# Attention with narrow products in double groups and three banks for each kind of scores, and a shorter gating search, lists and beginning

## The chip, the cores and the metric

The kernel runs on one core of a Trainium2 chip. The metric is the device time of one execution in microseconds (us). A core has a matrix engine (TensorE; PE in the profile, its weight loads PEld), a vector engine (VectorE, DVE), an activation engine (ScalarE, ACT), a general one (GpSimd, POOL), and a queue engine (SyncE, SP) that mostly issues DMAs. Each runs its own instructions in order and they meet only through semaphores. The matrix engine writes to eight banks of PSUM, 512 float32 numbers a partition each.

## The reference

Two layers over `x` of 16 x 256 x 512, with `ctx_2048` of the same shape: a long convolution over the context that stands for the first attention, a mixture of 32 small experts gated once per batch entry, a true attention, and a mixture of 8 experts with the two best for each row.

```
x = x + tanh(g_xattn[0]) * L0_xattn(ctx, ctx, layernorm(x), ssm_kernel, D, 8)
x = x + tanh(g_ffn[0])   * L0_ffn(layernorm(x), sim_matrix, gates, w_q, w_k, w_v, o_weights)
x = x + tanh(g_xattn[1]) * L1_xattn(layernorm(x), ctx, ctx)
x = x + tanh(g_ffn[1])   * L1_ffn(layernorm(x), w_router, w_fc, w_proj)

L0_ffn gating:  logits = affinity - sigmoid(gates); mask = relu(logits) > 0
                if no expert is active: the mask is that of the 16 largest logits of 32
                routing = softmax(where(mask > 0, gated, -max))
L1_xattn:       qk = einsum('bdm,bdn->bmn', qh, kh) / sqrt(32)   # 128 heads, each 512 x 512
                ret = einsum('bmn,bcn->bcm', softmax(qk), vh)
L1_ffn:         two best of 8 experts a row; y = square(relu(x @ w_fc[e])) @ w_proj[e], weighted
```

## The kernel before

The program runs as five stages: layer norm and transposes; the convolution as products with Toeplitz blocks; the gating and first experts; the attention with the routing of its rows; and the second experts, 71 tiles of 128 rows gathered by expert. The change touches three of them.

**Gating** (end of the third stage). DVE makes the logits of 16 batch entries and 32 experts, and finds which are among the 16 largest by comparing all pairs: five operations over 16x1024 (`over`, `same`, `rank`, L908 to L912). POOL made the triangle `later` for ties. From the mask come `rm` and `RB`, and PE's products L805 combine the experts' output weights, which SP loads at L610. PE runs a filler, `stir(pe, pk[5], 34)`, products with the identity that nothing reads, in the meantime.

**Attention.** The work is 32 units, each of four heads of 512 x 512. `unit_loop` runs `body(j, i, u)` with eight units written out and the rest as a loop of four. In a unit PE issues, in 16 beats, one *second* score product (L1463, keys against queries with the maxima as two more rows, 98 deep, for unit j) and one *first* score product (L1445, 96 deep, for a unit ahead, by `ahead` with `LEAD = 5` pairs of tiles). First scores go to `pA`, two pairs of banks: DVE takes the negated maximum over two tiles at once (`reduce`, L1817), so a pair of banks is free when its one reduction is. When all 16 are in, POOL splits the maxima in a high and a low part (`halves`), PE turns them (`maxima`, L1454) at beat `TURN = 10`, ACT copies them (`keep`, L1661), and SP moves them into two rows of the queries (`shift`, L1251), which unit j+1 needs at its first beat. Second scores go to `pB`, two banks in turn (`bank`); ACT takes the exponential of each (L1710) into `pt`, and the product two places on waits for it. There are 17 places a unit in that ring (`RING`), 16 seconds and the turned maxima. POOL adds three of the four key blocks of `pt` (L1399, L1404).

The *narrow* products are 32 columns wide, four heads side by side: `values` (L1473) for each of four key blocks, and `sums` (L1486) with ones, once over POOL's part sums and once over the last block. Each is a group of four products and is put by hand at a beat: values 0 at 13, values 1 at 15, and in the next unit values 2 at 2, sums at 5 and 7, values 3 at 10.

The beginning: SP loads keys, queries and values of units 0, 1 and 2 (six loads of 256 KB and a value tile of 256 KB each) on one queue; PE runs a filler of 32, then all 16 first scores of unit 0 and 10 of unit 1; SP's queue holds the shift of unit 0 behind these loads.

**Lists** (behind the attention). DVE picks the two best experts of each row in four groups, PE counts, and then eight chunks make the slot lists: DVE's `where` (L1934) and `what` (L1939), ACT's scaled copies (L1764), PE's sums (L1606). Ahead of them DVE makes the picks' weights (`weights`). Then ACT copies the first expert's weights (`fc_at`, L1771), SP having loaded all of them, and the tiles begin.

## Time and profile before

| | us |
|---|---|
| median of 3 runs | 1626.49 (1622.04 to 1628.45) |
| the profiled execution | 1629.35 |
| its span | 1627.3 |
| PE busy | 1538.0 (95%) |
| DVE busy | 1193.8 (73%) |
| POOL busy | 1032.7 (63%) |
| ACT busy | 980.1 (60%) |
| mean granted clock of PE | 0.978 |

The page shows each engine's busy time, the span in 40 slices, the DMA queues, the chain of work that ended last, and the costliest groups of instructions. A chain names, step by step, what released the work; with `<-` a row names the releaser of an idle time. The attention lies between about 525 and 1037 us of the span, the gating's end about 437 to 454, the lists about 1090 to 1118. Matmul ends are modelled, so a product's listed duration is longer than the distance to the next one's start; distances between starts are what counts.

### The profile page before, as it was taken

How to read it: one execution, taken by the hardware profiler on the slowest of the kernel's cores; microseconds unless marked ns; L12 is line 12 of the kernel's file. 1: busy time of each engine (PE TensorE's matmuls, PEld its weight loads, DVE VectorE, ACT ScalarE, POOL GpSimd, SP SyncE). 2: the span in 40 equal slices, each digit the busy share in tenths (PEclk: the TensorE clock that was granted, in tenths of full speed). 3: DMA queues.
4: the chain of work that ended last, by engine and by line, in shares of the span. 5: the costliest groups of instructions: out<-in, count | busy, mean ns of one | idle time of the engine just before them, and what ended most of it. 6: DMA issues, size and time to landing. Idle time of an engine off the chain costs nothing.

```text
span 1627.3 us, 28669 instructions
## 1 busy us (share of the span) xinstructions
PE 1538.0 (95%) x8969; PEld 1080.2 (66%) x8969; DVE 1193.8 (73%) x1869; ACT 980.1 (60%) x1529; POOL 1032.7 (63%) x855
## 2 busy tenths in 40 slices
PE   5999999998897999999999999888999999999996
PEld 4677777777653644444444444368999999999995
DVE  7688888888837677777777777166777777777774
ACT  6333333333724378888888887637667767777773
POOL 4788888885406588888888887501555555555553
PEclk9999999999998999999999999989999999999998
DMA  7244444445763967777777772491444444444443
GB/s 256 97 132 137 142 142 142 142 132 130 197 186 100 199 167 194 189 184 204 183 187 201 186 188 75 155 328 36 79 75 79 79 74 75 78 77 78 79 79 52
DMA packets 110843, 224.27 MB, mean 138 GB/s; under 512 B 12704, under 2 KB 12704, under 8 KB 109856
## 3 DMA queue, kind: packets, MB, share of 16 engines
q1 hardware_dynamic: 94848, 185.88, 40.4%
q0 software_dynamic: 15904, 37.23, 13.2%
q8 instruction: 49, 0.80, 0.2%
q14 instruction: 42, 0.34, 0.1%
HBM read 146.71 MB, written 75.84 MB: 137 GB/s over the span
## 4 chain that ended last, share of the span: by engine, by line
PE 38%; DMA 20%; issue 3%; DVE 3%; ACT 2%; POOL 1%; SPq 0%; ACTq 0%; POOLq 0%; DVEq 0%
DMA out_rows<-XN,slots 18%; PE pB L1463 10%; PE pO L1473 8%; PE pA L1445 7%; PE pO L1486 4%; PE pA L1624 3%; PE pO L1636 3%; DMA XN<-normed_rows,slots 1%; PE pB L1454 1%; PE pA L1541 1%; DVE low L1817 1%; POOL out_rows L1429 1%; PE pA L1614 1%; DMA qs<-q_low 1%; PE pA L1548 0%
## 5 line engine op out<-in xcount | busy, mean ns | idle before, releaser
L1817 DVE TENSOR_REDUCE low<-pA 128x2 f32<-128x1024 f32 x256 | 306.9, 1223 | 113.2 <-PE pA L1445 99.5
L1710 ACT ACTIVATE pt<-pB 128x512 f32<-128x512 f32 x512 | 287.6, 594 | 88.4 <-PE pB L1463 80.2
L436 PE MATMUL y<-kv,toep 128*128 128x288 f32 x1280 | 327.8, 413 | 9.1 <-DVEq L63 5.8
L1429 POOL DMA_INDIRECT out_rows<-XN,slots x71 | 195.2, 2749 | 211.9 <-DMA out_rows<-XN,slots 172.8
L436 PEld LDWEIGHTS y<-kv,toep 128*128 128x128 f32 x1280 | 239.1, 191 | 97.6 <-DVEq L63 34.1
L1624 PEld LDWEIGHTS pA<-XN,fc 128*128 128x128 f32 x2272 | 264.3, 192 | 7.9 <-issue 2.6
L1624 PE MATMUL pA<-XN,fc 128*128 128x128 f32 x2272 | 265.1, 275 | 2.0 <-issue 1.0
L1463 PE MATMUL pB<-qs,ks 98*128 98x512 f32 x512 | 226.8, 446 | 3.4 <-ACT pt L1710 2.4
L1463 PEld LDWEIGHTS pB<-qs,ks 98*128 98x128 f32 x512 | 95.3, 188 | 193.5 <-ACT pt L1710 150.5
L406 ACT ACTIVATE ym<-y 128x384 f32<-128x384 f32 (+1 forms) x128 | 52.6, 411 | 230.6 <-PE y L436 230.6
L1776 ACT ACTIVATE proj_high<-WP 128x2048 fp32r x71 | 135.7, 1912 | 81.2 <-PE pO L1636 81.2
L1445 PE MATMUL pA<-ks,qs 96*128 96x512 f32 x512 | 182.6, 399 | 0.5 <-DMA qs<-q_low 0.3
L1992 DVE TENSOR_TENSOR proj_low<-WP,proj_high 128x2048 fp32r<-128x2048 f32 x71 | 162.8, 2292 | 8.1 <-ACT proj_high L1776 3.0
L1399 POOL TENSOR_TENSOR part_sum<-pt 128x1024 f32<-128x1024 f32 x64 | 152.2, 2378 | 21.8 <-ACT pt L1710 16.0
L1404 POOL TENSOR_TENSOR part_sum<-part_sum,pt 128x1024 f32<-128x1024 f32 x64 | 152.6, 2385 | 6.9 <-POOL part_sum L1399 3.8
L1473 PE MATMUL pO<-pt,vt 128*32 128x512 f32 x1024 | 136.0, 604 | 0.0
L1771 ACT ACTIVATE fc<-WF 128x2048 f32 x71 | 134.4, 1894 | 0.8 <-issue 0.8
L374 POOL TENSOR_TENSOR R<-ym,qc 128x384 f32<-128x384 f32 (+1 forms) x128 | 99.3, 798 | 55.7 <-ACT ym L406 53.8
L157 POOL TENSOR_TENSOR kv<-kc 128x1024 f32<-128x1024 f32 x64 | 121.3, 1895 | 5.3 <-PEq L425 3.1
L1636 PE MATMUL pO<-proj_high,hh 128*128 128x512 f32 x284 | 118.7, 418 | 3.2 <-DVE proj_low L1992 3.2
L1091 POOL DMA_INDIRECT XN<-normed_rows,slots x71 | 72.1, 1015 | 75.1 <-DVEq L1981 53.8
L1997 DVE SCALAR_TENSOR_TENSOR XN<-pA,XN 128x512 f32<-128x512 f32 x71 | 49.1, 692 | 92.4 <-ACT XN L1781 92.4
(293 smaller groups left out, 2524.5 us busy)
## 6 DMA issues: line engine op xcount, KB each, us to landing
ks<-ctx_high SPq DMA_DIRECT2D x64, 256.0 KB, 4.6
qs<-q_high SPq DMA_DIRECT2D x64, 256.0 KB, 6.2
kc<-in_ctx_conv SPq DMA_DIRECT2D x32, 384.0 KB, 5.4
XN<-in_x SPq DMA_DIRECT2D x16, 512.0 KB, 9.7
toep<-kernel_and_skip SPq DMA_DIRECT2D x32, 256.0 KB, 3.5
ct<-in_ctx SPq DMA_DIRECT2D x16, 512.0 KB, 6.5
ctx_high<-kh SPq DMA_DIRECT2D x16, 512.0 KB, 4.4
ctx_low<-kl SPq DMA_DIRECT2D x16, 512.0 KB, 5.1
```

The source lines that it names most:

```text
L436: m = pe.matmul(y[half].rearrange("p (l n) c -> p l n c", l=CB)[:, l, :, 0:PAIRS], toep[u][:, (l - s) * P:(l - s + 1) * P], kv[u][:, half, ...
L1399: pool.tensor_tensor(part_sum[:, 2 * n:2 * n + 2], pt[0][:, 2 * n:2 * n + 2], pt[1][:, 2 * n:2 * n + 2], ALU.add).then_inc(s_add, 1)
L1404: pool.tensor_tensor(part_sum[:, 2 * n:2 * n + 2], part_sum[:, 2 * n:2 * n + 2], pt[2][:, 2 * n:2 * n + 2], ALU.add).then_inc(s_add, 1)
L1429: pool.indirect_dma_start(out=out["out"], out_offset=bass.IndirectOffsetOnAxis(ap=slots[:, j:j + 1], axis=0), in_=ys[j % 2], in_offset=Non ...
L1445: m = pe.matmul(pA[n % 2][:, half, :], qs[u][0:NS, h, m0:m0 + P].bitcast(F32R), ks[u][0:NS, h, :].bitcast(F32R), start=True, stop=True)
L1463: pe.matmul(bank(u, n), ks[u][0:NS + 2, h, s * P:(s + 1) * P].bitcast(F32R), qs[u][0:NS + 2, h, :].bitcast(F32R), start=True, stop=True).t ...
L1473: m = pe.matmul(pO[u % 2][h * HD1:(h + 1) * HD1, :], vt[u][:, s, h * HD1:(h + 1) * HD1], pt[s][:, h, :], start=(s == 0), stop=(s == CB - 1))
L1624: m = pe.matmul(pH[j % 2][:, b * P:(b + 1) * P], fc[j % 2][:, k * C + b * P:k * C + b * P + P], xc[j % 2][:, k * P:(k + 1) * P], start=(k ...
L1636: m = pe.matmul(pY[j % 2], picks[j % 2][:, rows].bitcast(F32R), proj[:, weights].bitcast(F32R), start=(k == 0 and n == 0), stop=(k == CB - ...
L1710: act.activation(pt[s][:, h, :], bank(u, n), ACT.Exp, scale=SCALE1).then_inc(s_exp, 1)
L1817: dve.tensor_reduce(ap(low[u % 2], t % CB * NH + t // CB, [[NH, 2], [1, 1]]), pA[n % 2], op=ALU.max, axis=AX.X, negate=True).then_inc(s_re ...
L1992: dve.tensor_tensor(wpl.bitcast(F32R), ap(WP, e, [[1, CB * C]]), wph[j % 2], ALU.subtract).then_inc(s_low, 1)
```

## The change

In the attention, first scores use three single banks (`scores_to`) and each 128x512 tile has a reduction of its own; second scores use three banks (`seconds_to`), one of them the fourth half of `pA`. The narrow groups stand in pairs: values 0 and 1 at beat 13, values 2 and 3 at beat 2 and both sums at beat 7 of the next unit. Unit 0 is loaded by heads, partly from ACT; unit 0's shift is issued ahead of unit 2's loads; only four scores of unit 1 come before unit 0's second scores and twelve in its first six beats. The gating's search is two rounds of `max` and `match_replace`; the triangle is gone. In the lists, the weights are made partly while DVE waits for the totals and partly on POOL, the chunks come in another order, and PE waits for each scaled copy rather than for eight. Three fillers are shorter, and one of 14 and one of 6 are new.

```diff
-                stir(pe, pk[5], 34)
+                stir(pe, pk[5], 20)
...
                 dve.wait_ge(s_con, CONS)
-                mine = ap(t["logits"], 0, [[1, E0], [0, E0]])
-                other = ap(t["logits"], 0, [[0, E0], [1, E0]])
-                chain.inc(dve.tensor_tensor(over, other, mine, ALU.is_gt))
-                chain.link(dve.tensor_tensor(same, other, mine, ALU.is_equal))
-                chain.link(dve.tensor_tensor(same, same, later, ALU.mult))
-                chain.link(dve.tensor_tensor(over, over, same, ALU.add))
-                chain.link(dve.tensor_reduce(t["rank"], over, op=ALU.add, axis=AX.X))
-                chain.link(dve.tensor_scalar(t["rank"], t["rank"], float(FALLBACK), cnt, ALU.is_lt, ALU.mult))
+                values = t["logits"]
+                for n in range(FALLBACK // 8):
+                    chain.link(dve.max(best[n], values))
+                    chain.link(dve.match_replace(left[n], best[n], values, -FMAX))
+                    values = left[n]
+                chain.link(dve.tensor_scalar(t["rank"], values, -FMAX, cnt, ALU.is_equal, ALU.mult))
...
-        DUOS = TILES // 2
         RING = TILES + 1
         TURN = 10
         LEAD = 5
+        FIRST = 2
+        CATCH = 2 * (LEAD - FIRST)
+        HEADS = [(0, 1), (1, 2), (2, NH)]
...
-        def bank(u, n):
-
-            return pB[(u * RING + n) % 2]
+        scores_to = [pA[0][:, 0], pA[0][:, 1], pA[1][:, 0]]
+        seconds_to = [pB[0], pB[1], pA[1][:, 1]]
+
+        def score_bank(t):
+
+            return scores_to[t % 3 if t < TILES - 1 else 1]
+
+        def score_earlier(j, t):
+
+            return TILES * j + (t - 3 if 3 <= t < TILES - 1 else {0: -4, 1: -1, 2: -2, TILES - 1: TILES - 3}[t]) + 1
+
+        def bank(n):
+
+            return seconds_to[n % 3]
+
+        def bank_earlier(j, n):
+
+            return made(j, n - 3) if n >= 3 else made(j - 1, {0: RING - 2, 1: RING - 1, 2: RING - 3}[n])
...
-            for u in range(3):
-                load(u, u)
+            first_keys(0)
+            first_queries(0)
+            first_keys(1)
+            first_keys(2)
+            sp.wait_ge(s_head[1], 16 * LOADS)
+            load(1, 1)
+            load_values(0, 0)
+            shift(0, 0)
+            load(2, 2)
+            for u in (1, 2):
                 load_values(u, u)
-            shift(0, 0)
...
+            rows_roots()
...
+            def weights():
+                pool.wait_ge(s_gap, GROUPS + 1)
+                chain.link(pool.tensor_scalar(weight[:, :, 0], wgt, gates[:, 3:4], None, ALU.mult))
+                chain.link(pool.tensor_tensor(weight[:, :, 1], weight[:, :, 0], e2, ALU.mult))
+                pool.sem_inc(s_gap, 1)
+
+            weights()
...
-                n, half = t // 2, t % 2
-                if t == 0:
+                if isinstance(j, int) and j == 0 and t // CB in (0, 1, 2) and t % CB == 0:
+                    pe.wait_ge(s_head[t // CB], 16 * LOADS)
+                elif t == 0:
                     pe.wait_ge(s_ld[u], 16 * LOADS * i + 16 * LOADS)
-                if half == 0:
-                    wait(pe, s_red, DUOS * j + n - 1)
+                wait(pe, s_red, score_earlier(j, t))
                 h, m0 = t // CB, t % CB * P
-                m = pe.matmul(pA[n % 2][:, half, :], qs[u][0:NS, h, m0:m0 + P].bitcast(F32R), ks[u][0:NS, h, :].bitcast(F32R),
-                              start=True, stop=True)
-                if half:
-                    m.then_inc(s_a, 1)
+                pe.matmul(score_bank(t), qs[u][0:NS, h, m0:m0 + P].bitcast(F32R), ks[u][0:NS, h, :].bitcast(F32R),
+                          start=True, stop=True).then_inc(s_a, 1)
...
-                wait(pe, s_exp, made(j, n - 2))
-                pe.matmul(bank(u, n), ks[u][0:NS + 2, h, s * P:(s + 1) * P].bitcast(F32R), qs[u][0:NS + 2, h, :].bitcast(F32R),
+                if isinstance(j, int) and j == 0 and n < 3:
+                    wait(pe, s_exp, n % 2)
+                else:
+                    pe.wait_ge(s_exp, bank_earlier(j, n))
+                pe.matmul(bank(n), ks[u][0:NS + 2, h, s * P:(s + 1) * P].bitcast(F32R), qs[u][0:NS + 2, h, :].bitcast(F32R),
                           start=True, stop=True).then_inc(s_b, 1)
...
                 if beat == 2:
                     values(j, i, u, 2)
-                if beat == 5:
+                    values(j, i, u, 3)
+                if beat == 7:
                     sums(j, u, False)
-                if beat == 7:
                     sums(j, u, True)
-                if beat == 10:
-                    values(j, i, u, 3)
+
+            def onward(j, i, u, beat):
+
+                if isinstance(j, int) and j == 0 and beat < CATCH:
+                    for t in range(2 * (FIRST + beat), 2 * (FIRST + beat) + 2):
+                        score(1, 0, 1, t)
+                else:
+                    score(*ahead(j, i, u, beat))
...
             def body(j, i, u):
                 before = following(j, i, u, -1)
                 for beat in range(TILES):
                     if beat in (2, 5, 13):
-                        score(*ahead(j, i, u, beat))
+                        onward(j, i, u, beat)
                     if beat == TURN and exists(j + 1):
                         score(*ahead(j, i, u, beat))
-                        wait(pe, s_exp, made(j, TURN - 2))
-                        maxima(j + 1, bank(u, TURN))
+                        pe.wait_ge(s_exp, bank_earlier(j, TURN))
+                        maxima(j + 1, bank(TURN))
                     second(j, u, beat // NH, beat % NH)
                     if beat not in (2, 5, TURN, 13):
-                        score(*ahead(j, i, u, beat))
+                        onward(j, i, u, beat)
...
                     if beat == 13:
                         values(j, i, u, 0)
-                    if beat == 15:
                         values(j, i, u, 1)
 
...
-            stir(pe, idle, 32)
+            stir(pe, idle, 12)
...
+            stir(pe, idle, 6)
             maxima(0, pB[1])
             pe.wait_ge(s_one, 6)
-            for t in range(2 * LEAD):
+            for t in range(2 * FIRST):
                 score(1, 0, 1, t)
...
+            stir(pe, pT[0], 14)
...
-                pe.wait_ge(s_W, c + 1)
                 for n in range(G):
+                    pe.wait_ge(s_W, G * c + n + 1)
...
+            for g in (1, 2):
+                lo, hi = HEADS[g]
+                for n, src in enumerate((QHu, QHu, QLu)):
+                    act.dma_start(qs[0][n * HD1:(n + 1) * HD1, lo:hi], src[0][:, lo:hi]).then_inc(s_head[g], 16)
...
-            act.wait_ge(s_w, 1)
+            act.wait_ge(s_gap, GROUPS + 2)
...
-            act.wait_ge(s_wf, 16 * E1)
+            act.wait_ge(s_weights, 32 * E1)
...
-                for beat in range(1, TILES, 2):
-                    to = ahead(j, i, u, beat)
-                    reduce(*to[:3], to[3] // 2)
+                for beat in range(TILES):
+                    if isinstance(j, int) and j == 0 and beat < CATCH:
+                        for t in range(2 * (FIRST + beat), 2 * (FIRST + beat) + 2):
+                            reduce(1, 0, 1, t)
+                    else:
+                        reduce(*ahead(j, i, u, beat))
...
+                dve.wait_ge(s_e2, 1)
+                link(dve.tensor_scalar(wgt, e2, 1.0, None, ALU.add))
+                dve.reciprocal(wgt, wgt).then_inc(s_gap, 1)
...
-            def weights():
-                dve.wait_ge(s_e2, 1)
-                link(dve.tensor_scalar(wgt, e2, 1.0, None, ALU.add))
-                link(dve.reciprocal(wgt, wgt))
-                link(dve.tensor_scalar(weight[:, :, 0], wgt, gates[:, 3:4], None, ALU.mult))
-                link(dve.tensor_tensor(weight[:, :, 1], weight[:, :, 0], e2, ALU.mult))
-                dve.sem_inc(s_w, 1)
...
+            what(0)
+            for c in range(1, CHUNKS):
+                if c >= CHUNKS // 2:
+                    places(c)
+                where(c)
                 what(c)
-                if c < CHUNKS // 2:
-                    places(CHUNKS // 2 + c)
             link(dve.tensor_tensor(above, ap(count[0:1], 0, [[1, TILES9], [0, E1]]),
                                    ap(t8["incl"][0:1], 0, [[0, TILES9], [1, E1]]), ALU.is_ge))
```

## Rows read from the trace of the kernel before

**Rows 1.** The chain of waits between 700 and 800 us, its shares by line.

```profile
by line: PE pB L1463 33.4%; PE pO L1473 26.9%; PE pA L1445 24.4%; PE pO L1486 12.9%; PE pB L1454 2.6%
```

**Rows 2.** Timeline of PE in one unit: start us, us, engine, line, operation, count.

```profile
752.70 0.42 PE L1463 MATMUL pB<-qs,ks 98*128 98x512 f32 x1
753.05 1.06 PE L1486 MATMUL pO<-part_sum,ones 128*32 128x512 f32 x8
754.04 0.50 PE L1463 MATMUL pB<-qs,ks 98*128 98x512 f32 x1
754.38 0.40 PE L1445 MATMUL pA<-ks,qs 96*128 96x512 f32 x1
754.62 0.40 PE L1463 MATMUL pB<-qs,ks 98*128 98x512 f32 x1
...
768.24 1.07 PE L1486 MATMUL pO<-part_sum,ones 128*32 128x512 f32 x8
```

**Rows 3.** Timeline of PE: two narrow groups back to back.

```profile
1039.98 1.06 PE L1486 MATMUL pO<-part_sum,ones 128*32 128x512 f32 x8
1040.86 1.04 PE L1486 MATMUL pO<-pt,ones 128*32 128x512 f32 x8
```

**Rows 4.** One tile's instructions (ns min/median/max): a reduction of 128x512 from PSUM.

```profile
L881 DVE TENSOR_REDUCE ssum<-pk x1: 693/693/693, 436.6 to 436.6; 128x1 f32<-128x512 f32 x1
```

**Rows 5.** Timeline in unit 0: reductions, a score that waited for one, the next product.

```profile
558.51 2.36 DVE L1817 TENSOR_REDUCE low<-pA 128x2 f32<-128x1024 f32 x2 [0.60 <-PE pA L1445]
...
559.79 0.50 PE L1445 MATMUL pA<-ks,qs 96*128 96x512 f32 x1 [0.20 <-DVE low L1817]
...
560.13 0.60 PE L1454 MATMUL pB<-ident,split 128*8 128x128 f32 x4
```

**Rows 6.** Timeline of PE and ACT in one unit: maxima, their copy, exponentials, a root.

```profile
757.46 0.60 PE L1454 MATMUL pB<-ident,split 128*8 128x128 f32 x4
...
758.17 0.59 ACT L1661 ACTIVATE tops<-pB 8x512 fp32r<-8x512 f32 x1 [0.37 <-PE pB L1454]
...
759.82 1.08 ACT L1710 ACTIVATE pt<-pB 128x512 f32<-128x512 f32 x2
...
762.92 0.19 ACT L1680 ACTIVATE guess<-lnv 128x1 f32<-128x1 f32 x1
```

**Rows 7.** Timeline of ACT in unit 31: idle before, and its releaser.

```profile
1025.14 1.78 ACT L1710 ACTIVATE pt<-pB 128x512 f32<-128x512 f32 x3 [0.83 <-PE pB L1463]
```

**Rows 8.** Timeline at the attention's beginning: first shift, first second scores of units 0 and 1.

```profile
547.60 1.38 SPq L1251 DMA_DIRECT2D qs<-tops  x2
...
553.10 0.50 PE L1463 MATMUL pB<-qs,ks 98*128 98x512 f32 x1 [0.47 <-DMA qs<-tops]
...
566.14 0.50 PE L1463 MATMUL pB<-qs,ks 98*128 98x512 f32 x1
```

**Rows 9.** Windows: stretch, busy us by engine, PEclk, DMA share, GB/s.

```profile
440.00:445.00 5.00, 4.71 (x34) 4.69 (x35) 3.12 (x13) 0.46 (x2) 0.00 (x0) 0.50 1.00 210
540.00:545.00 5.00, 5.00 (x37) 4.50 (x35) 5.00 (x5) 0.00 (x0) 0.00 (x0) 1.00 1.07 229
```

**Rows 10.** Timeline in the gating: a search operation, and the product behind the gating.

```profile
443.91 1.21 DVE L908 TENSOR_TENSOR WM<-logits 16x1024 f32<-16x1024 f32 x1
...
453.43 8.94 PE L805 MATMUL pk<-XN,RB 128*64 128x512 f32 x20 [0.95 <-DVEq L927]
```

**Rows 11.** One line's DMAs, the experts' output weights: issues, and time to landing.

```profile
L610 SPq DMA_DIRECT2D XN<-in_w_o x4: 350/422/493, 429.2 to 430.5; - x4
...
DMA to landing us min/median/max: 7.7/15.6/21.6
```

**Rows 12.** Timeline of the lists and the first tile: weights, ACT's copy, columns.

```profile
1092.95 0.18 DVE L1926 TENSOR_SCALAR wgt<-e 128x32 f32<-128x32 f32 x1
...
1115.78 3.71 ACT L1771 ACTIVATE fc<-WF 128x2048 f32 x2 [0.81 <-issue]
...
1123.63 0.68 DVE L1986 COPY XN<-pA 128x512 f32<-128x512 f32 x1
```

More of the change, by code:

```diff
@@ L541, in _build @@
             ones = sb(st, "ones4", [P, B])
-            later, over, same = (WM[0:B].rearrange("p b k h -> p (b k h)")[:, n * E0 * E0:(n + 1) * E0 * E0]
-                                 .rearrange("p (e f) -> p e f", f=E0) for n in range(3))
+            best = [sb(st, f"best{i}", [B, 8]) for i in range(FALLBACK // 8)]
+            left = [sb(st, f"left{i}", [B, E0]) for i in range(FALLBACK // 8)]
             eg = sb(st, "eg", [B, E0])
@@ L1956, in _ @@
             tables()
-            weights()
             dve.wait_ge(s_xe, 16 * TRIP)
```

78 lines of the change are left out of this document (36 added, 42 removed).

## The prediction

> **What bounds the kernel now.** I read the page's slices first (five stages with different fillings), then the chain of waits over a stretch of the attention, then the timeline of one attention unit with PE and ACT side by side. The chain between 700 and 800 us stays on PE alone: it names five PE lines and no releaser [rows 1]. The reader is to see that PE waits for nobody there, so a unit takes the sum of PE's issue intervals. That sum closes: the same narrow product starts at 753.05 and at 768.24, a period of 15.19 us [rows 2]; 32 wide products at 0.24, six groups of narrow ones at 0.99, 0.10 to 0.11 more on each side of a group, and 0.41 for the turned maxima give 15.2. Anything that makes PE wait in a unit is therefore paid about 30 times.
>
> **Doubling the narrow groups.** A wide product starts 0.35 before a narrow group rather than 0.24, the next wide one 0.99 after its start, and the one behind that 0.34 later [rows 2]. Two groups back to back start 0.88 apart [rows 3]. A pair in place of two single groups saves 0.11 + 0.10 + (0.99 - 0.88), about 0.33; three pairs a unit save 1.0 us. POOL's partial sums come earlier in relation to their reader (beat 7 for 5), so that wait stays covered.
>
> **What the new banks make PE wait for.** The reduction is split: one of 128x512 from PSUM took 0.69 [rows 4], against 1.23 for 1024 and 1.18 from start to start [rows 5]. I take 0.64 from start to start (0.69 less the same 0.05 of overlap): 16 of them are 10.2 us a unit against 8 x 1.18 = 9.4. DVE has room (about 13 of 15.2), but its latency now stands in PE's way. Scores go round three banks, and 16 is no multiple of 3: score 15 takes the bank of score 13, two back, and so is its only cover two products. Laid out from the end of the pair at beat 2: second at 0, score 13 at 0.34, second 0.58, score 14 at 0.82, and score 15, put ahead of its second at beat 5, is due at 1.05. Score 13 ends 0.40 after its start, DVE starts 0.03 later, ends at 0.34 + 0.43 + 0.69 = 1.46, and PE resumes 0.05 behind a reduction's end [rows 5]: 1.52. Wait 0.47. A product that had to wait is followed by the next after 0.34, not 0.24 [rows 5], so 0.10 more: 0.57.
> The ring of second scores has 17 places over 3 banks, and places 0 and 1 of a unit again stand two behind. Beat 0 is due at 1.05 after the pair of beat 13; the exponential of beat 14 starts at 0.53 (the first product behind a group takes 0.50), takes 0.59 [rows 6] and releases at 1.18: 0.13 + 0.10. The next one follows it by 0.49 and a root of 0.19 [rows 6], so ends at 1.8 and releases at 1.85 where beat 1 is due at 1.76: 0.09 + 0.10. The maxima take place 10, and place 13 waits for their copy: 0.71 to the copy's start and 0.59 in it [rows 6], 1.35 with the release; place 13 is due at 1.22 now that no narrow group stands between: 0.13 + 0.10. Together 1.22 lost and 1.0 gained: +0.22 a unit, a period of 15.4; over 30 units +6.6. Bounds: no wait bites, -1.0 a unit, -30; every wait at the long end of its rows (0.03 longer release, DVE at 0.66, each with its feedback), +0.55, +17. I take the middle because each of its pieces has a row of its own, and the same pieces give the 15.19 of before.
> *The Trainium skill* (Advanced Engine Details and Errata, The Read-Write Bubble) says large tiles are to be preferred because the access latency is paid per instruction; its Perfetto Trace Analysis (Optimizing Scalar/DVE Operations) puts it at about 125 ns for DVE on PSUM, by which eight more reductions would cost 1.0 us of DVE, where the rows give 0.8. The same section says that splitting may let work be completed sooner where DVE is not saturated and makes bubbles elsewhere; by that rule alone the change would win the whole 30 us, which is the first rival.
>
> **The last two units** run without scores and on ACT's pace, and ACT stands still 0.83 behind a narrow group [rows 7]. About seven such gaps (5.5 us) become four or five of about 1.0 with a third bank: -1.5 (0 to -3).
>
> **The beginning of the attention.** Now the first score waits for all six loads of unit 0. The shift of the maxima is issued at 547.60, and the first second score starts at 553.10 [rows 8], behind the loads that sit ahead of the shift in SP's queue. Loaded by heads and issued from two engines, head 0 needs 0.4 MB; six issues and a landing put the first score near 530.5, an estimate. Sixteen reductions at 0.64 end at 541.2, the shift is issued 2.0 later (as now) at 543.1 and, with only two units loaded ahead of it, lands near 545.4. That is 7.7 earlier. Then it is given back twice. Unit 0 has 12 scores in six beats and is DVE's: 22 reductions, about 15 us instead of 13.0. And the DMA engines are full in this stretch (share 1.07 at 229 GB/s in 540 to 545 [rows 9]). Between the first shift and unit 1's shift SP's queue holds the loads of units 2 and 3 (1.57 MB each), two value tiles (0.52) and the query stores (0.52): 4.2 MB, about 19 us, none of which may start before 545. Unit 1's shift lands near 566.5, and unit 1's first second score starts there, against 566.14 now [rows 8]. So +0.5; bounds -4.5 (the queue isn't what is late) and +2. The Trainium skill (DMA: Bandwidth & Descriptors, Issuing engines are not separate DMA queues) says that issuing from several engines saves only issue time, since the same 16 engines run it all; the trace's full share over this stretch agrees, and no run here shows two issuers.
>
> **Gating.** Five operations over 1024 elements at 1.21 [rows 10] go, some 6.3 us with their links; two pairs of maximum-of-eight and replacement come, which the trace doesn't show. On 32 elements the neighbours take 0.14 to 0.24, on 1024 it is 1.21; nearest by size are the small ones, 0.25 each with the link, 1.0 together. The routing matrix is ready 5.2 earlier, near 448.2. But the product that uses it waits for the expert weights too, and the last of their four loads is issued at 430.5 and lands up to 21.6 later [rows 11]: 452.1, and the product starts at 453.43 now [rows 10], 1.3 behind. So -1.3 rather than -5.2. The filler of 20 instead of 34 ends near 448, an estimate from its present end at 451, and PE then stands for some 4 us. PE's clock was at 0.50 in 440 to 445 [rows 9], after PE had stood for about half of the 5 us ahead. If it falls there again, from 2.4 to 1.2 GHz, the first of the products, 0.89 each (20 records, two to a product, in 8.94 [rows 10]), run at half speed: +2 for some 4 us of that. Term: +0.7 (2.0 - 1.3), bounds -5.2 and +4.
>
> **The lists.** Four operations of the weights leave DVE's path, from 1092.95 [rows 12] to the next work 1.2 later; two of their four operations go into DVE's wait for the totals, two to POOL. PE starts its chunks sooner (eight chunks of about 2.0 from the first value list on) and would end them some 3.7 earlier, but the last value list comes 0.2 later than before in relation to the first, and what follows is a queue on ACT and DVE: first expert's weights at 1115.78, two more copies of 1.9, the low half on DVE, and only then the first columns at 1123.63 [rows 12], which stand behind that low half in DVE's order. That chain moves by 1.2 less 0.2 and a shorter end on ACT: -1.3 (0 to -3.7). The expert stage behind it only shifts.
>
> **Sum.** 6.6 - 1.5 + 0.5 + 0.7 - 1.3 = +5.0. The profiled execution took 1629.35 (span 1627.3 and 2.05 around it), 2.9 over the median 1626.49; that difference is not of a part that changes, so I put the sum on the median: **1631.5 us**.
>
> **Rivals.**
> *All waits are covered* (chance 0.15). For it: splitting the reduction frees a bank sooner, and DVE and ACT have 15 to 20% of slack. Against it: score 15 is due 0.47 before its bank can be free by single rows. -30 and the other terms -1.6: 1595.
> *Only score 15 waits* (0.15). If ACT's releases come some 0.15 sooner than I laid out, a unit takes -1.0 + 0.57 = -0.43, -13 in all: 1612.
> *The waits feed on each other* (0.25), the slower side. PE starts late, so the engines behind it do, and place 0 and 13 wait again; ACT's pace rather than PE's sets a beat, as where second scores already followed ACT in unit 0. It decides as soon as the four waits come to more than 1.4 a unit; at the long ends +0.55 a unit: +17 and -1.6, 1642, and as much again on the ranges of the beginning and the gating, up to 1648.
> *The forecast* (0.45), its own range 1624 to 1640.
>
> **Numbers.** A measurement of this kernel tells about 0.5%, 8 us, from no change. Of the forecast's 0.45 some 0.32 lie within that and 0.10 above it, 0.03 below; the first two rivals are faster (0.30), the third slower (0.25). That gives 0.33 faster, 0.32 same, 0.35 slower. The range for 8 in 10 reaches into both sides: 1600 to 1648.
>
> **What would show it.** A unit's period in the steady stretch: 15.4, with PE idle ahead of one score a unit (0.5, released by the reduction) and three second scores (0.1 each, released by ACT); 14.2 would show the first rival, 15.7 the third. Pairs of narrow groups 1.87 long. Unit 1's first second score at its old distance from the stage's start, waiting for the shift. The gating product released by the weights' load, with the clock's lower level over its first products. The first columns in the expert stage behind the low half. The forecast is wrong if score 15 doesn't wait.

## The result, and the profile after

The changed kernel took **1634.96 us** (median of 5 runs, 1634.61 to 1638.19) against 1626.49 (5 runs, 1622.04 to 1628.45): a ratio of 1.0047, interval 1.0026 to 1.0069. It is slower by about half a per cent, 3.5 us above the forecast of 1631.5. Timed again later it took 1631.71 (10 runs) against 1628.19, a ratio of 1.0020 (1.0002 to 1.0038). Its profiled execution has a span of 1632.8 us, 5.5 more than before.

The first view is TensorE in one steady unit, to be laid beside [rows 2]; first and second scores are now lines L1477 and L1496, the values L1506 and the sums L1519.

```profile
752.21 0.40 PE L1496 MATMUL pB<-qs,ks 98*128 98x512 f32 x1
752.45 0.40 PE L1477 MATMUL pA<-ks,qs 96*128 96x512 f32 x1
753.15 0.50 PE L1477 MATMUL pA<-ks,qs 96*128 96x512 f32 x1 [0.31 <-DVE low L1858]
753.50 0.40 PE L1496 MATMUL pA<-qs,ks 98*128 98x512 f32 x1
...
754.44 0.50 PE L1477 MATMUL pA<-ks,qs 96*128 96x512 f32 x1
754.87 1.06 PE L1519 MATMUL pO<-part_sum,ones 128*32 128x512 f32 x8
755.75 1.04 PE L1519 MATMUL pO<-pt,ones 128*32 128x512 f32 x8
756.72 0.50 PE L1496 MATMUL pA<-qs,ks 98*128 98x512 f32 x1
...
758.89 0.39 PE L1477 MATMUL pA<-ks,qs 96*128 96x512 f32 x1
759.36 0.50 PE L1496 MATMUL pB<-qs,ks 98*128 98x512 f32 x1
...
763.16 0.39 PE L1477 MATMUL pA<-ks,qs 96*128 96x512 f32 x1
763.54 0.50 PE L1496 MATMUL pB<-qs,ks 98*128 98x512 f32 x1
763.88 0.40 PE L1477 MATMUL pA<-ks,qs 96*128 96x512 f32 x1
764.12 0.50 PE L1496 MATMUL pB<-qs,ks 98*128 98x512 f32 x1
764.46 0.63 PE L1477 MATMUL pA<-ks,qs 96*128 96x512 f32 x2
```

Read the starts, not the durations: two wide products with nothing between start 0.24 apart. Score 15 starts 0.70 behind score 14, so it waited 0.46, and the next one follows it by 0.35. Place 13 (759.36) is 0.47 behind its forerunner and place 0 (763.54) 0.38: waits of 0.23 and 0.14, too short for this view to print a releaser. Place 1 (764.12) shows only the long form, 0.50 in its duration and 0.34 to its follower, and so does score 1, which also takes the bank of two scores back (754.44: 0.50, and the pair of sums follows by 0.43 where 0.33 is usual). The pair of narrow groups takes 1.85 to the next product (754.87 to 756.72).

The costliest groups between 700 and 1000 us show the new reduction, and that one line of TensorE now stands idle for it:

```profile
L1858 DVE TENSOR_REDUCE low<-pA 128x1 f32<-128x512 f32 x310 | 198.4, 685 | 43.6 <-PE pA L1477 35.3 <-DVE mv L1882 6.5
...
L1477 PE MATMUL pA<-ks,qs 96*128 96x512 f32 x311 | 117.5, 408 | 6.0 <-DVE low L1858 6.0
```

and the chain of waits over the same stretch, which was TensorE alone in [rows 1], has VectorE and ScalarE in it:

```profile
by line: PE pO L1506 24.4%; PE pA L1477 24.2%; PE pB L1496 20.8%; PE pO L1519 11.7%; PE pA L1496 7.8%; DVE low L1858 4.7%; PE pB L1484 2.8%; ACT tops L1705 2.6%; issue 1.0%; ACTq L1704 0.2%
```

The gating and its clock, against [rows 9, 10]: the second and last replacement now ends at 442.3 (the last comparison ended at 450.0), and the product waits for the experts' output weights. First its timeline, then the windows, with columns as in [rows 9]:

```profile
445.81 0.25 PE L790 MATMUL pk<-ident,rm 16*32 16x16 f32 x8
449.67 10.57 PE L799 MATMUL pk<-XN,RB 128*64 128x512 f32 x20 [3.62 <-DMA XN<-in_w_o]
```

PEclk, third from the end, is 0.66 under the first products, after 3.6 us of standing. The 0.59 in 440 to 445 isn't the shorter filler's doing: TensorE was at its filler (438.5 to 445.9) all through it, and before, with the long one, it was 0.50 there.

```profile
440.00:445.00 5.00, 5.00 (x29) 5.00 (x29) 3.44 (x21) 0.41 (x2) 0.00 (x0) 0.59 1.01 205
445.00:450.00 5.00, 1.38 (x17) 1.03 (x17) 0.68 (x4) 0.00 (x0) 0.00 (x0) 1.00 0.51 105
450.00:455.00 5.00, 5.00 (x9) 1.38 (x8) 0.00 (x0) 1.77 (x3) 0.00 (x0) 0.66 0.00 0
```

The beginning of the attention, a timeline against [rows 8]:

```profile
541.78 1.38 SPq L1269 DMA_DIRECT2D qs<-tops  x2
...
544.50 0.50 PE L1496 MATMUL pB<-qs,ks 98*128 98x512 f32 x1 [1.08 <-DMA qs<-tops]
...
562.89 0.50 PE L1496 MATMUL pB<-qs,ks 98*128 98x512 f32 x1 [0.67 <-DMA qs<-tops]
```

The end of the lists and the first expert tile, against [rows 12]:

```profile
1116.92 3.71 ACT L1814 ACTIVATE fc<-WF 128x2048 f32 x2 [1.26 <-DVEq L2014]
...
1120.93 0.62 PE L1654 MATMUL pA<-ident,XN 128*128 128x128 f32 x4
...
1122.56 2.29 DVE L2030 TENSOR_TENSOR proj_low<-WP,proj_high 128x2048 fp32r<-128x2048 f32 x1 [5.23 <-ACT proj_high L1819]
1124.77 0.68 DVE L2024 COPY XN<-pA 128x512 f32<-128x512 f32 x1
...
1125.60 2.73 PE L1664 MATMUL pA<-XN,fc 128*128 128x128 f32 x16 [4.05 <-DVE XN L2024]
```

For the whole I cut both traces at the same events. Differences after less before, us:

| stretch | before | after | difference | forecast |
|---|---|---|---|---|
| start to the members' product (code unchanged but for POOL's triangle) | 438.3 | 436.1 | -2.2 | |
| members' product to the attention's first DMA (gating) | 86.7 | 87.1 | +0.35 | +0.7 |
| first DMA to the first sums (beginning) | 45.4 | 46.4 | +1.05 | +0.5 |
| the next 28 units | 426.0 | 432.3 | +6.3 | +6.6 |
| the last three units | 43.5 | 39.8 | -3.7 | -1.5 |
| first turn to the first down product (lists, first tile) | 94.9 | 96.0 | +1.1 | -1.3 |
| first down product to the end (code unchanged) | 494.8 | 497.6 | +2.7 | |

("First turn" is the first transpose of the attention's output rows behind the scores; it starts 2.4 us ahead of the last sums in both, so that the stretches overlap by that much.)

### The profile page after: what moved, and what is told of

It is laid out like the page before. It is cut to its first block, busy times and chain, and to the rows that moved or that the text cites. A ratio compares the mean times of both kernels' runs of the same rounds, so it can differ in the third digit from the quotient of the medians.

```text
span 1632.8 us, 29206 instructions
## 1 busy us (share of the span) xinstructions
PE 1528.0 (94%) x8923; PEld 1081.1 (66%) x8923; DVE 1209.9 (74%) x2124; ACT 966.5 (59%) x1529; POOL 1033.0 (63%) x855
## 4 chain that ended last, share of the span: by engine, by line
PE 32%; DMA 24%; DVE 5%; issue 4%; ACT 2%; POOL 1%; SPq 0%; ACTq 0%; POOLq 0%; DVEq 0%
DMA out_rows<-XN,slots 22%; PE pO L1506 7%; PE pA L1477 7%; PE pB L1496 6%; PE pO L1519 4%; PE pA L1496 2%; DVE low L1858 2%; PE pO L1676 1%; DMA XN<-normed_rows,slots 1%; PE pA L1664 1%; PE pB L1484 1%; ACT tops L1705 1%; PE pA L1580 1%; POOL out_rows L1461 1%; DVE XN L2044 0%
## 5 line engine op out<-in xcount | busy, mean ns | idle before, releaser
L1858 DVE TENSOR_REDUCE low<-pA 128x1 f32<-128x512 f32 x512 | 327.2, 685 | 83.6 <-PE pA L1477 71.6
L1461 POOL DMA_INDIRECT out_rows<-XN,slots x71 | 198.6, 2797 | 216.9 <-DMA out_rows<-XN,slots 166.4
L1754 ACT ACTIVATE pt<-pB 128x512 f32<-128x512 f32 x352 | 194.5, 591 | 51.6 <-PE pB L1496 51.4
L1477 PE MATMUL pA<-ks,qs 96*128 96x512 f32 x512 | 196.6, 417 | 10.8 <-DVE low L1858 10.4
L2030 DVE TENSOR_TENSOR proj_low<-WP,proj_high 128x2048 fp32r<-128x2048 f32 x71 | 162.7, 2292 | 10.4 <-ACT proj_high L1819 5.2
L1496 PE MATMUL pB<-qs,ks 98*128 98x512 f32 x352 | 155.5, 444 | 4.3 <-DMA qs<-tops 1.7
L1496 PEld LDWEIGHTS pB<-qs,ks 98*128 98x128 f32 x352 | 66.8, 190 | 99.2 <-ACT pt L1754 65.8
L1754 ACT ACTIVATE pt<-pA 128x512 f32<-128x512 f32 x160 | 94.3, 589 | 59.5 <-PE pA L1496 59.4
L1477 PEld LDWEIGHTS pA<-ks,qs 96*128 96x128 f32 x512 | 98.3, 193 | 46.6 <-DVE low L1858 34.1
L1506 PE MATMUL pO<-pt,vt 128*32 128x512 f32 x1024 | 123.3, 598 | 0.1
```

The lines of the kernel that those rows point to most:

```text
L1461: pool.indirect_dma_start(out=out["out"], out_offset=bass.IndirectOffsetOnAxis(ap=slots[:, j:j + 1], axis=0), in_=ys[j % 2], in_offset=Non ...
L1477: pe.matmul(score_bank(t), qs[u][0:NS, h, m0:m0 + P].bitcast(F32R), ks[u][0:NS, h, :].bitcast(F32R), start=True, stop=True).then_inc(s_a, 1)
L1496: pe.matmul(bank(n), ks[u][0:NS + 2, h, s * P:(s + 1) * P].bitcast(F32R), qs[u][0:NS + 2, h, :].bitcast(F32R), start=True, stop=True).then ...
L1506: m = pe.matmul(pO[u % 2][h * HD1:(h + 1) * HD1, :], vt[u][:, s, h * HD1:(h + 1) * HD1], pt[s][:, h, :], start=(s == 0), stop=(s == CB - 1))
L1754: act.activation(pt[s][:, h, :], bank(n), ACT.Exp, scale=SCALE1).then_inc(s_exp, 1)
L1858: dve.tensor_reduce(ap(low[u % 2], t % CB * NH + t // CB, [[1, 1]]), score_bank(t), op=ALU.max, axis=AX.X, negate=True).then_inc(s_red, 1)
```

## The experiments

"Period" is the mean distance of the sums' first product over 20 to 23 steady units; it is 15.20 in the kernel before and 15.45 in the changed one.

**The change again, and two orders of the banks.** The first kernel is the changed one as it is.

> The changed kernel once more, unchanged, to see how far stages without an edit move between two profiled executions. If the expert stage's 2.7 us over the kernel before (497.6 against 494.8 us from the first down product to the end) are chance, it gives them back here and the profiled span comes out within about 3 us of 1632.8; if they belong to the changed kernel (the order of its code or buffers), the stage is 497 to 498 us again. The attention's period should be 15.47 us a unit in either case.

Measured: 1631.71 us (10 runs), period 15.45, expert stage 494.9. So those 2.7 us were chance; over all profiles taken the stage scatters from 491.6 to 497.6 with nearly the same code, the stretch up to the members' product from 435.4 to 438.3. A single difference of spans tells nothing below some 4 us, the stretches with an edit tell more.

The second changes only which bank a score takes.

```diff
+        SCORE_BANK = (0, 2, 1, 0, 2, 1, 0, 2, 0, 1, 2, 0, 1, 0, 2, 1)
         def score_bank(t):
-            return scores_to[t % 3 if t < TILES - 1 else 1]
+            return scores_to[SCORE_BANK[t]]
          def score_earlier(j, t):
-            return TILES * j + (t - 3 if 3 <= t < TILES - 1 else {0: -4, 1: -1, 2: -2, TILES - 1: TILES - 3}[t]) + 1
+            return TILES * j + t - back(SCORE_BANK, t) + 1
```

(`back` finds the last use of the same bank, so many scores ago.)

> The changed kernel with one thing changed: the order in which a unit's 16 score tiles go round their three banks, so that no tile takes the bank of the tile two before it at tile 15 (the turns of two places back fall at tiles 8 and 13 in place of 15 and 1, where a double group or the maxima lie between). Theory: the 0.46 us that the sixteenth score waits for the reduction two before it, with the 0.10 of its own weight load behind the wait, is all that makes a unit 15.47 instead of about 14.9 us; the period falls to 14.85 to 14.95 and the whole to about 1617 us (31 x 0.57 less than 1635). Rival: the reductions, 0.69 us each and one per beat, leave VectorE no slack, so that the wait moves on to another score and the period stays above 15.2 us, the whole above 1627 us. Second rival: ScalarE (a unit's 16 exponentials and the rest come to about 14.7 us of busy time in my sum) binds right away: 15.0 to 15.1, the whole 1621 to 1625 us.

Measured: **1612.28 us** against 1628.19, ratio 0.9899 (0.9868 to 0.9931), period **14.76**. In the groups between 700 and 1000 us TensorE's line of first scores has no idle time left:

```profile
L1483 PE MATMUL pA<-ks,qs 96*128 96x512 f32 x323 | 114.9, 396 | 0.0
```

The theory holds, both rivals fall; the gain is larger than expected (14.85 to 14.95 us a unit, about 1617). The unit is 0.69 shorter, more than the 0.46 + 0.10 of score 15, because the new order also takes score 1 off the bank of two scores back: its long form was another 0.10. Two turns of two places back remain, at scores 8 and 13, but each has a double group between.

The third kernel re-orders the places of the second scores as well.

```diff
+        SECOND_BANK = (0, 1, 2, 0, 1, 0, 2, 1, 0, 2, 1, 0, 2, 1, 0, 1, 2)
         def bank(n):
-            return seconds_to[n % 3]
+            return seconds_to[SECOND_BANK[n]]
```

> As the kernel with the re-ordered score banks, and the seventeen places of the second scores go round their banks in another order too: the places that take the bank of two places back are 5 and 15 in place of 0 and 1. Theory: the waits of places 0 and 1 (0.13 and 0.09 us, with 0.10 each for the weight load behind them) go, a smaller one comes at the double group of beat 2 or at place 13, and the period is another 0.15 us shorter, 14.7 us, the whole about 1612 us. Rival: at 14.85 us ScalarE is the bound and the wait moves to another place; then this kernel equals the one with the score banks alone within 2 us.

Measured: **1606.98 us**, ratio 0.9850 (0.9823 to 0.9876), period 14.65. The turns of places 0 and 1 had cost 0.24 and 0.10 and are gone, but a new wait comes. Of the two first scores in this timeline's first row, the second starts at 757.36, 0.36 behind the first, and has the long form: 0.12 and 0.10. So this order is worth only 0.11 a unit.

```profile
757.00 0.86 PE L1485 MATMUL pA<-ks,qs 96*128 96x512 f32 x2
757.70 0.40 PE L1504 MATMUL pA<-qs,ks 98*128 98x512 f32 x1
```

**Pairs and banks, each alone.** First the kernel before with the three double groups only.

```diff
                 if beat == 2:
                     values(j, i, u, 2)
-                if beat == 5:
-                    sums(j, u, False)
+                    values(j, i, u, 3)
                 if beat == 7:
+                    sums(j, u, False)
                     sums(j, u, True)
-                if beat == 10:
-                    values(j, i, u, 3)
 ...
                     if beat == 13:
                         values(j, i, u, 0)
-                    if beat == 15:
                         values(j, i, u, 1)
```

> The kernel before with one part of the change alone: its narrow groups run as three double groups a unit (behind second scores 2, 7 and 13) in place of six single ones; two banks for second scores and double tiles for first scores stay. What the pairing saves on TensorE is 3 x 0.33 us a unit, so theory 1 (TensorE's own work sets the period, 15.19 us) gives 14.2 to 14.4 us a unit and a whole near 1602 us; theory 2, the one that I hold, is that with two banks a double group of 1.85 us starves ScalarE, whose exponential wants a new tile every 0.5 to 0.6 us, so that the two second scores after it wait, and the period falls by no more than half of that: 14.7 to 15.2 us, the whole 1611 to 1627 us.

Measured: **1669.66 us** against 1628.19, ratio 1.0251 (1.0214 to 1.0289), period **16.48**. Both expectations missed: it isn't a smaller gain, it is a loss of 1.3 us a unit. The timeline of TensorE around one double group, and behind it that of ScalarE:

```profile
755.04 0.49 PE L1463 MATMUL pB<-qs,ks 98*128 98x512 f32 x1
756.02 0.50 PE L1463 MATMUL pB<-qs,ks 98*128 98x512 f32 x1 [0.48 <-ACT tops L1658]
...
757.45 0.50 PE L1463 MATMUL pB<-qs,ks 98*128 98x512 f32 x1
757.88 1.92 PE L1473 MATMUL pO<-pt,vt 128*32 128x512 f32 x16
759.74 0.50 PE L1463 MATMUL pB<-qs,ks 98*128 98x512 f32 x1
...
760.55 0.40 PE L1445 MATMUL pA<-ks,qs 96*128 96x512 f32 x1
760.93 0.50 PE L1463 MATMUL pB<-qs,ks 98*128 98x512 f32 x1
```

```profile
758.30 0.57 ACT L1707 ACTIVATE pt<-pB 128x512 f32<-128x512 f32 x1
758.78 0.28 ACT L1674 ACTIVATE lnv<-mv,eps 128x1 f32<-128x1 f32 x1
760.28 0.60 ACT L1707 ACTIVATE pt<-pB 128x512 f32<-128x512 f32 x1 [1.22 <-PE pB L1463]
```

During the group only the second score issued ahead of it is left for ScalarE, whose exponential is done at 758.9; ScalarE stands 1.22 us. Then it is behind and TensorE waits for it: 760.93 is a second score 0.38 behind its forerunner. A ring of two has no tile in store for 1.85 us. The largest single wait has another reason: the second score at 756.02 starts 0.98 behind the one before it, because it takes the bank of the turned maxima, two places back, and waits for ScalarE's copy of them; in the kernel before the group of beat 10, now moved to beat 2, stood between. Between 700 and 1000 us TensorE waits for this copy 18 times. With its long form that wait is about 0.8 of the 2.3 us that the unit lies above 14.2. How much of the rest is the pairs' length alone no run separates.

Next the banks alone: the changed kernel with the same lines of the last diff put back to single groups.

> The changed kernel with its narrow groups single again, at the six places where the kernel before has them, so that with the runs before it the table of pairing and third banks is full (neither 15.19, pairs alone 16.48, both 15.46 us a unit). If pairing and banks only add up, the third banks by themselves are worth 15.46 - 16.48 = -1.0 and this kernel makes 14.2 us a unit. Theory: it can't, because without pairs TensorE's own work is 3 x 0.33 us more and the sixteenth score still waits for the reduction two before it, now without a double group's 1.85 us between: my sum gives 15.4 us of work with 0.5 to 0.8 us of wait, 15.9 to 16.1 us a unit, the whole 1645 to 1655 us. So both parts alone would be losses and only together nearly even.

Measured: 1637.88 us against 1624.18, ratio 1.0083 (1.0063 to 1.0103), period 15.75, 0.15 below the theory's lower end; the whole is below its 1645 to 1655 too. The timeline of TensorE in a unit shows the same wait, now 0.52 (0.76 less 0.24):

```profile
754.86 0.40 PE L1477 MATMUL pA<-ks,qs 96*128 96x512 f32 x1
755.62 0.50 PE L1477 MATMUL pA<-ks,qs 96*128 96x512 f32 x1 [0.36 <-DVE low L1861]
```

So the two parts don't add: alone +1.28 and +0.55 a unit, together +0.25. The fourth corner puts single groups under the re-ordered banks.

> The kernel with both rings re-ordered, its narrow groups single at the six places of the kernel before. It asks what pairing is worth once no bank is reused two places back at a bad place. Theory: 3 x 0.33 us of TensorE's time, less the small waits that the pairs leave (0.2 to 0.3 us): 15.2 to 15.4 us a unit against 14.65, the whole 1625 to 1632 us. Rival: a single group is long enough for ScalarE and VectorE to catch up everywhere, a double one starves them; then it is below 15.0 us.

Measured: 1621.28 us (10 runs) against 1624.18, ratio 0.9980 (0.9968 to 0.9991), period 15.14, just below the theory's 15.2 to 15.4 and above the rival's 15.0. Periods in a table:

| us a unit | single groups | double groups |
|---|---|---|
| two banks, double tiles (before) | 15.20 | 16.48 |
| three banks, order of the change | 15.75 | 15.45 |
| three banks, re-ordered | 15.14 | 14.65 |

With good banks the pairing is worth 0.49, not the 1.0 that its issue intervals give: half of it comes back as short waits. In a unit with pairs and both orders changed these are two, 0.23 at place 13 for the maxima's copy and 0.12 at the score shown above, each with 0.10 behind it, 0.55 together; in a unit with single groups the timeline shows neither. And good banks without pairs give 0.06, because TensorE waited for nobody in [rows 1].

**Gating and first tile.** Two edits on the kernel with both orders changed.

```diff
-                stir(pe, pk[5], 20)
+                stir(pe, pk[5], 34)
 ...
-            proj_low(0)
             columns(0)
+            proj_low(0)
             columns(1)
```

> The kernel with both rings re-ordered and two edits in other stages. First, 34 transposes of filler ahead of the gating product again, with the new search kept: in the changed kernel the granted clock there is 0.59 in 440 to 445 us with 20 transposes. If the clock costs what it seems to, the members' product to the first DMA of the attention becomes 1 to 2 us shorter than with 20 (85.3 to 87.3 us in five profiles); if the loads of w_o bind, the gating product stays 13.6 to 13.9 us behind the members' product and nothing is gained. Second, VectorE copies the first expert tile's columns before, not after, it makes the first low weights: in the changed kernel the transposed tile lies ready at 1121.55 us and its copy starts at 1124.77, TensorE idles 4.05 us and runs the first up product at a lower clock (2.73 instead of 2.02 us). Theory: the copy starts within 0.3 us of the transposes, and from the first turn to the first down product it takes 92.5 to 94 us instead of 95.8 to 96.5; rival: the low weights, now later, hold the first down product and nothing is gained. The whole 1603 to 1606 us if both come, 1607 if none does.

Measured: 1601.44 us against 1624.18, ratio 0.9860 (0.9833 to 0.9887), another chip than the 0.9850 above, so the totals don't separate the two edits' gain; the stretches do. (Timed again on the first chip, in the run below, this kernel has 0.9859, no less than the 0.9850 without the edits. So that the whole gains by the two edits isn't shown.) In the gating the product still starts 13.8 behind the members' product, behind the weights' load, but the twenty records take 8.91 instead of 10.57 (timeline), and the granted clock stays up (windows, columns as before):

```profile
449.27 8.91 PE L799 MATMUL pk<-XN,RB 128*64 128x512 f32 x20 [2.05 <-DMA XN<-in_w_o]
```

The row to read is the last, 1.00 under the products where the changed kernel had 0.66; in 440 to 445 the filler was running in both:

```profile
440.00:445.00 5.00, 5.00 (x44) 5.00 (x44) 2.89 (x19) 0.41 (x2) 0.00 (x0) 0.93 0.88 179
445.00:450.00 5.00, 2.95 (x29) 2.34 (x28) 0.68 (x4) 0.00 (x0) 0.00 (x0) 1.00 0.25 52
450.00:455.00 5.00, 5.00 (x13) 1.09 (x11) 0.00 (x0) 3.23 (x6) 0.00 (x0) 1.00 0.22 29
```

All 32 records of this product take 14.7 to 14.8 us in each of the six profiles with 34 transposes and 16.0 to 17.4 in each of the seven with 20. The stage takes 83.9 us (83.8 and 83.9 in two more profiles with this gating, 85.2 in a third; 85.3 to 87.9 with 20 transposes). In the first tile the copy follows the transposes, and the up product runs at full speed (timeline):

```profile
1094.13 0.66 PE L1662 MATMUL pA<-ident,XN 128*128 128x128 f32 x4
...
1094.83 0.69 DVE L2032 COPY XN<-pA 128x512 f32<-128x512 f32 x1 [4.39 <-PE pA L1662]
...
1095.67 2.02 PE L1672 MATMUL pA<-XN,fc 128*128 128x128 f32 x16 [0.88 <-ACT proj_high L1827]
...
1095.85 2.29 DVE L2038 TENSOR_TENSOR proj_low<-WP,proj_high 128x2048 fp32r<-128x2048 f32 x1 [0.33 <-ACT proj_high L1827]
```

First turn to first down product is 90.6 us (89.8, 91.3 and 87.1 in the later profiles) against 95.6 to 96.8 in every profile with the new lists and without the swap: more than the 2 to 3.5 us expected. From the first up to the first down product it takes 8.0 us in all four with the swap, as in the kernel before, and 9.65 to 10.4 in all with the new lists and without it.

**The beginning.** First on the kernel with both orders changed: `FIRST = LEAD`, loads of units 0 to 2 ahead of the shift, 32 transposes of filler.

> The kernel with both rings re-ordered, its beginning of the attention as in the kernel before (all of units 0 to 2 loaded in whole units ahead of the first row of maxima, ten scores of unit 1 ahead of the first second score, 32 transposes of filler, the roots' rows first on GpSimd). The new beginning brings unit 0's first second score 6.7 us forward, unit 1's 1.4 us, and the first sums not at all (46.4 and 45.8 us behind the attention's first DMA against 45.3). Theory: both beginnings end in the same queue of loads, so the first sums come 45 to 46 us behind the first DMA and the whole is 1605 to 1608 us; rival: with the faster steady units the early start counts in full and this one is 3 to 6 us slower.

Measured: 1608.44 us against 1624.18, ratio 0.9904 (0.9877 to 0.9932). The first sums came at 45.4, as the theory had it; the attention took 491.7 against 496.2. But the ratio is higher than the 0.9850 with the new beginning (0.9823 to 0.9876), timed on the other chip: by the totals the old beginning is, if anything, the slower one here. Then three kernels, timed together on one chip. The best so far once more:

> The kernel with both rings re-ordered, 34 transposes ahead of the gating product and the first columns copied ahead of the first low weights, once more and in more rounds, as what the two below are compared with. 1598 to 1604 us; a steady unit 14.65 us, first turn to first down product 90.5 to 91.5 us, members' product to attention 83.5 to 85 us.

with the old beginning:

> The same with the attention's beginning of the kernel before. In single profiles the attention (first DMA to first turn) took 491.7 us with the old beginning and 493.7 to 496.2 us with the new one, at the same 14.65 us a unit. Theory 1: that is the beginning's doing, since with early starts unit 1's rows of maxima land behind three units' loads; then this kernel is 2 to 4 us faster than the one above. Theory 2: it is the scatter of where loads land in one execution; then the two medians agree within 1.5 us.

and with unit 1's shift issued by ScalarE:

```diff
                             keep(j + 1, bank(TURN), made(j, TURN))
+                            if isinstance(j, int) and j == 0:
+                                act.wait_ge(s_exp, made(0, TURN))
+                                for row in range(2):
+                                    part = tops[row * NH:(row + 1) * NH]
+                                    act.dma_start(qs[1][NS + row:NS + row + 1], bass.AP(part.tensor, part.offset, [list(part.ap[0]), [C, 1], [1, C]])).then_inc(s_md, 16)
```

> The same as the first of these three, with the two transfers that bring unit 1's row of maxima under its queries issued from ScalarE's queue in place of SyncE's. Unit 0's rows land 2.7 us after their issue, with the transfer engines at 0.13 of their time, unit 1's 4.9 us and later, with the engines at 1.05, and unit 1's first second score waits up to 2.07 us for them. If the wait is the order of SyncE's own queue, the rows land about 2.7 us after their issue again, the wait goes and the first sums come 1 to 2 us sooner; if the 16 transfer engines are simply full, another queue changes nothing: they land 4 to 5 us after their issue, and the whole agrees within 1.5 us.

Measured: 1606.07 (1600.21 to 1607.27), 1601.51 (1596.31 to 1603.91) and 1603.78 (1601.09 to 1606.91) against 1628.89; ratios 0.9859 (0.9835 to 0.9883), 0.9831 (0.9806 to 0.9856) and 0.9859 (0.9837 to 0.9880). The first is 2 us above its expected range. The old beginning is 4.6 lower in the median and its attention 1.6 us shorter in the profile (492.1 against 493.7), but the intervals overlap, and the pair of ratios above (0.9904 old, 0.9850 new) points the other way. Which beginning is the better one stays open; the profiles show only that the new one brings the first sums no sooner once both orders are changed and the groups are pairs (47.0 to 49.8 in four profiles, 45.4 and 45.8 with the old one). For the shift from ScalarE the windows show how busy the transfer engines were:

```profile
556.00:558.00 2.00, 1.52 (x6) 0.64 (x4) 1.83 (x4) 0.51 (x1) 1.92 (x2) 1.00 1.07 206
558.00:560.00 2.00, 0.94 (x9) 0.41 (x13) 0.62 (x2) 1.59 (x4) 0.96 (x2) 1.00 1.04 288
560.00:562.00 2.00, 2.00 (x19) 0.78 (x12) 0.00 (x0) 0.60 (x2) 2.00 (x1) 1.00 0.60 218
```

They are full until 560 whoever issues (1.05 in 558 to 560 with SyncE's shift, 1.04 with ScalarE's). When the rows moved the trace tells too, because they are the only transfers in this stretch on ScalarE's queue (q10 in the DMA view): issued from 556.53 on, all 16 of its packets lie between 560.7 and 561.2, up to 4.6 us behind, and SyncE's queue took 103% of the engines from 558.4 to 560.7. That is the expectation's second case, the engines are full, and not the 2.7 us of its first. The wait for the rows at unit 1's first second score is gone from the timeline, but ScalarE's 1.82 us of issuing holds an exponential, TensorE waits 1.54 for it, and that score starts 40.9 behind the first DMA instead of 41.3; the first sums come at 47.0 instead of 47.3. What the Trainium skill (DMA: Bandwidth & Descriptors, Issuing engines are not separate DMA queues) says, that another issuer saves issue time alone, fits these packets; but here the issuing was dear, for it stood on an engine with work.

## Why the prediction was right

**The waits at the banks** came as laid out: score 15 waits 0.46 (predicted 0.47), place 0 0.14 (0.13), place 13 0.23 (0.13), place 1 nothing but its long form (0.09), each with about 0.10 behind it; the period is 15.45 for 15.41. The reduction takes 0.685, a pair and its follower 1.85 for 1.87. That it was these waits is shown by taking them away by bank order alone. Two things the layout missed. Score 1 also stands two back and has the long form, 0.10, which is why removing the 0.56 of score 15 gave 0.69. And removing the turns of places 0 and 1 gave 0.11 for the 0.42 that I had put on them: they measure 0.34, and 0.22 of that comes back as the wait of a first score.

**"All waits are covered"** was the rival for the whole 1.0 us a unit. Even with both orders good the unit takes 14.65, 0.45 above its 14.2. The rival came from a rule of the Trainium skill (Perfetto Trace Analysis, Optimizing Scalar/DVE Operations): where VectorE isn't saturated but makes other engines stand, splitting its instructions may let work be completed sooner. A split reduction is indeed done sooner (0.685 us instead of 1.23), but the rule's condition was not met: in [rows 1] TensorE stood for nobody, and the waits came only with the new banks.

**The last units** gained 3.7 instead of 1.5 us, beyond the bound of 3. With single groups under the good banks the last three intervals add to 40.6, with pairs under the change's to 39.8, and to 43.5 before: most of it is the third bank, not the pairing. The way there was not the one that I had counted: ScalarE's idle time in these intervals falls only from 11.0 to 9.8, TensorE's waits from 3.2 to 1.6 (both in pieces above 0.15 us); where the rest comes from stays open.

**The beginning** went as argued: the first second score of unit 0 comes 6.7 us sooner (21.3 for 28.0 behind the first DMA; the estimate was 7.7), unit 1's 1.4 sooner (forecast: 0.5 later), and by the first sums nothing is left (+1.05, and +0.4 in the second profile). It is given back within unit 0: between the two second scores lie 18.4 us, where I had put about 15 and the kernel before has 13.05. The DMA engines are at 1.05 to 1.08 from 545 to 560, which is where the loads of units 2 and 3 run, and unit 1's first second score waits for the shift as forecast, 0.67. TensorE also ran a piece of unit 0 at half clock (0.65 in 545 to 550 and 0.50 in 550 to 555), which I had not foreseen. The clock doesn't decide it: the kernel with both orders changed has 1.00 in both stretches, takes 17.7 for the same piece and has its first sums at 49.8; there TensorE waits 2.07 for the shift.

**The gating** was right in both halves: the product waits for the weights' load (13.6 behind the members' product for 15.1, -1.5 for -1.3), and the shorter filler lets the clock fall (10.57 for 8.94, +1.6 for +2.0).

**The lists are the step that failed**: -1.3 forecast, +1.1 and +1.6 measured. The front was right, the columns come 0.6 sooner; but I let the chain end there. Counted from the first turn, the tile's transposes start after 81.7 us instead of 85.3, but their copy stands behind the low weights on VectorE, as I had said, and comes at 85.5 instead of 86.1. What follows from that I missed: TensorE, which had 0.97 us of idle time ahead of the first up product before, now stands 4.05 and the clock falls to 0.67 in 1125 to 1130. The up product takes 2.73 for 2.02, and from its start to the first down product it takes 9.65 for 8.01: that 1.6 less the 0.6 is the +1.1. The swap of two lines takes that away and lets the 3.6 us through. One caution: the old lists scatter too, 94.9 in the kernel before and 93.4 in the kernel with pairs alone, whose lists are the same.

**The sum** of the stretches that change is +5.0, the forecast's own number, and that is luck in part: the lists were forecast 2.4 too low and the last units 2.2 too high. The median's +8.5 in one comparison and +3.5 in another is that with the scatter of unchanged stretches.

## What to carry to other kernels

In a ring of n buffers whose uses per round are no multiple of n, some turns must be short: write the order as a table and put each short turn where the longest other work lies between; here that was worth 25 us of 1632 for two tuples of numbers. Longer uninterrupted groups and deeper buffering belong together, and testing either alone would have thrown both away. Work brought forward is worth what the next instruction in the reader's own order allows, so follow it one engine further than where the gain appears, and look at the clock behind every idle stretch that the gain opens.

## What the runs showed of the hardware

- A wide product that had to wait, even for less than 0.25 us, is followed by the next after 0.33 to 0.35 instead of 0.24 (the changed kernel, 752 to 765 us); it shows as 0.50 instead of 0.40 in its duration, which finds waits too short for a releaser to be printed.
- Issuing two transfers of 8 KB from ScalarE's queue took 1.82 us there, 1.20 to 1.38 from SyncE's.
- Such a pair of transfers reached its reader 2.7 us after its issue with the transfer engines at 0.13 of their time (the changed kernel, 541.78 to 544.50), 4.9 us after it with the engines at 1.08 in 558 to 560 (558.02 to 562.89); from ScalarE's queue, with the engines at 1.04 to 1.07, its packets were through after 4.6 us.
